# The first mean stage of a four-layer graph network: h computed by nodes in one product, with its bias, instead of by features and then turned

## What is computed

```python
# layer 2 and the norm behind it
out = fts @ W_l.T + aggregate @ W_r.T
out = out / norm(out, axis=1)
x = _layernorm(x + out)
# layer 3 starts with
h = x @ lin_w.T + lin_b
```

## Time and profile before

| | us |
|---|---|
| median of 3 runs | 5813.14 (5809.81 to 5825.58) |
| the profiled execution, its own time | 5838.2 |
| its span, from first to last instruction | 5836.3 |
| TensorE (PE) busy | 4153.4 |
| VectorE (DVE) busy | 3937.3 |
| POOL busy | 3517.6 |
| ScalarE (ACT) busy | 2806.0 |
| mean granted TensorE clock | 0.87 of full |

### The profile page before, as it was taken

How to read it: one execution, slowest core, us unless ns; L and a number is a source line. 1 busy time by engine, 2 the same in 40 slices (tenths; PEclk the granted TensorE clock), 3 DMA queues, 4 the chain that set the end, 5 groups by cost and what they waited for, 6 DMA issues and landing times. The chain is left out here.

```text
span 5836.3 us, 75364 instructions
## 1 busy us (share of the span) xinstructions
PE 4153.4 (71%) x16190; PEld 2475.1 (42%) x16190; DVE 3937.3 (67%) x13570; ACT 2806.0 (48%) x6338; POOL 3517.6 (60%) x3137
## 2 busy tenths in 40 slices
PE   5666649999994556466664779967996679756654
PEld 2333335555552333244442445534443334346643
DVE  6567759999995444277774885557666888746533
ACT  0434438788881100176663445534444555446543
POOL 4676658888866888545555650056105858855455
PEclk8788869999997777688886999989998999878776
DMA  6223333333323344456664774467545667657521
GB/s 219 73 80 83 78 74 110 114 110 113 112 91 73 62 62 63 68 179 196 200 195 131 209 209 136 123 190 217 152 142 163 188 172 210 188 186 229 169 79 53
DMA packets 785242, 802.39 MB, mean 137 GB/s; under 512 B 138080, under 2 KB 551848, under 8 KB 784666
## 3 DMA queue, kind: packets, MB, share of 16 engines
q1 hardware_dynamic: 403802, 393.43, 23.0%
q0 software_dynamic: 117504, 209.42, 14.9%
q10 hardware_dynamic: 263488, 194.72, 10.2%
HBM read 445.32 MB, written 351.92 MB: 137 GB/s over the span
## 5 line engine op out<-in xcount | busy, mean ns | idle before, releaser
L476 PE MATMUL gate_bank<-gate_ht,gate_whh 128*128 128x512 f32 x1764 | 884.9, 616 | 65.8 <-DVE gate_n L546 40.6
L942 POOL DMA_INDIRECT xh<-mean_xh,mean_pos_all x392 | 377.8, 964 | 342.5 <-DVE mean_xh L1008 209.6
L476 PEld LDWEIGHTS gate_bank<-gate_ht,gate_whh 128*128 128x128 f32 x1764 | 327.7, 197 | 469.3 <-issue 371.4
L2080 PE MATMUL back_ps_sums<-back_same,back_rows 128*128 128x512 f32 x400 | 288.8, 888 | 288.8 <-DMA back_rows<-x_a,back_idx 288.8
L1463 POOL DMA_INDIRECT ffn_rows<-att_sums,ffn_idx x392 | 394.4, 1006 | 124.0 <-issue 108.2
L291 POOL DMA_INDIRECT gate_rows<-h_a,by_pos x200 | 199.4, 997 | 428.9 <-POOLq L118 326.5
L472 PE MATMUL gate_bank<-by_rank,gate_win 128*128 128x512 f32 x882 | 435.3, 593 | 0.4 <-DVE by_rank L355 0.4
L612 ACT ACTIVATE gate_n<-gate_n,gate_b_ih 128x512 f32<-128x512 f32 x294 | 212.1, 722 | 397.0 <-issue 246.2
L1515 PE MATMUL ffn_ps_f<-ffn_hg,ffn_f 128*128 128x512 f32 x784 | 388.9, 597 | 3.0 <-ACT ffn_hg L1698 2.7
L1508 PE MATMUL ffn_ps_u<-ffn_xs_t,ffn_up_w 128*128 128x512 f32 x784 | 386.7, 595 | 1.1 <-issue 1.1
L2061 POOL DMA_INDIRECT back<-back_out,back_dest x200 | 324.4, 1622 | 67.8 <-issue 60.1
(11 more groups left out here) (270 smaller groups left out, 11751.2 us busy)
## 6 DMA issues: line engine op xcount, KB each, us to landing
mean_x<-x_a SPq DMA_DIRECT2D x196, 256.0 KB
back<-blank ACTq DMA_DIRECT2D x99, 264.0 KB, 4.4
mean_rows<-back SPq DMA_DIRECT2D x98, 264.0 KB
hp<-mean_xh SPq DMA_DIRECT2D x98, 264.0 KB
gate_x<-xh SPq DMA_DIRECT2D x98, 264.0 KB
gate_hot<-hot_rows SPq DMA_DIRECT2D x100, 256.0 KB
ffn_x<-in_x_in SPq DMA_DIRECT2D x98, 256.0 KB
ffn_xr<-in_x_in SPq DMA_DIRECT2D x98, 256.0 KB
```

What stands on the lines that cost most here:

```text
L476: last = nc.tensor.matmul(bank_[:, :], whh[:, c * D:(c + 1) * D], ht[:, t.slot4, :], start=not inputs, stop=True)
L942: nc.gpsimd.indirect_dma_start(out=g["xh"][:, :], out_offset=bass.IndirectOffsetOnAxis(ap=pos_all[:, t.n, j:j + 1], axis=0), in_=xh[:, t.n ...
L2080: last = nc.tensor.matmul(ps_sums[t.slot][:, :], rows[:, t.slot4, j, :], same[:, t.slot, j, :], start=j == 0, stop=j == J - 1)
```

## The change

h is made by nodes at once. TensorE first fills the bank `ps_h` with the bias by a product of a row of 128 ones (stationary, one partition) and lin_b repeated four times (moving, 1 x 512), then adds four products in which 128 turned rows of y are stationary and lin_w moves. ScalarE copies the bank into the finished row. The matmul by features, the bank `ps_ht`, the buffer `ht`, the turning back and VectorE's copy go. `ps_h` has two banks. The lags shrink: the columns 128 to 130 at 8 on VectorE (with the two setup copies that it makes ahead of tile 0's), the copy of h at 9 on ScalarE, POOL's indirect DMAs and the store of `hp` at 10. `lin_b` is loaded as one row of 512 floats in place of one number for each partition.

```diff
         @block.sync
-                if t := tile_at(11):
+                if t := tile_at(10):
                     wait(sp, id_done, t.n + 1)
                     wait_alone(sp, h_done, t.n + 1)
                     sp.dma_start(g["hp"]...)
         @block.gpsimd
-                if t := tile_at(11):
+                if t := tile_at(10):
         @block.tensor
             pe.wait_ge(w_loaded, 48)
+            pe.wait_ge(ones_set, 1)
...
                 if t := tile_at(8):
                     wait(pe, yt_done, t.n + 1)
-                    wait(pe, ht_done, t.n)
-                    nc.tensor.matmul(ps_ht[:, :], lin[:, :], yt[:, t.slot, :], start=True,
-                                     stop=True).then_inc(ht_made, 1)
-                if t := tile_at(9):
-                    wait(pe, ht_done, t.n + 1)
-                    wait(pe, h_done, t.n)
-                    for j in range(J):
-                        last = nc.tensor.transpose(ps_h[:, j * D:(j + 1) * D], ht[:, t.slot, j * P:(j + 1) * P],
-                                                   g["ident"][:, :])
-                    last.then_inc(h_turned, 1)
+                    wait(pe, h_done, t.n - 1)
+                    nc.tensor.matmul(ps_h[t.slot][:, :], ones[:, :], lin_b[:, :, :].rearrange("a j d -> a (j d)"),
+                                     start=True, stop=False, skip_group_check=True)
+                    for j in range(J):
+                        last = nc.tensor.matmul(ps_h[t.slot][:, j * D:(j + 1) * D], yt[:, t.slot, j * P:(j + 1) * P],
+                                                lin[:, :], start=False, stop=True, skip_group_check=True)
+                    last.then_inc(h_made, 1)
         @block.vector
+            nc.vector.memset(ones[:, :], 1.0).then_inc(ones_set, 1)
...
-                if t := tile_at(10):
-                    wait(dve, h_turned, t.n + 1)
+                if t := tile_at(8):
                     wait(dve, scattered[t.n % STAGED], 64 * (t.n // STAGED))
                     wait(dve, h_stored[t.n % STAGED], 16 * (t.n // STAGED))
...
                     nc.vector.tensor_copy(xh[:, t.n % STAGED, :, D:D + 3], tails[:, t.n, :, :]).then_inc(id_done, 1)
-                    nc.vector.tensor_copy(xh[:, t.n % STAGED, :, 0:D],
-                                          ps_h[:, :].rearrange("p (j d) -> p j d", j=J)).then_inc(h_done, 1)
         @block.scalar
                 if t := tile_at(9):
-                    wait(act, ht_made, t.n + 1)
-                    wait(act, h_turned, t.n - 1)
-                    nc.scalar.activation(ht[:, t.slot, :], ps_ht[:, :], ACT.Identity,
-                                         bias=lin_b[:, :]).then_inc(ht_done, 1)
+                    wait(act, h_made, t.n + 1)
+                    wait(act, scattered[t.n % STAGED], 64 * (t.n // STAGED))
+                    wait(act, h_stored[t.n % STAGED], 16 * (t.n // STAGED))
+                    nc.scalar.activation(xh[:, t.n % STAGED, :, 0:D],
+                                         ps_h[t.slot][:, :].rearrange("p (j d) -> p j d", j=J),
+                                         ACT.Copy).then_inc(h_done, 1)
                 if t := tile_at(8):
                     wait(act, y_turned, t.n + 1)
-                    wait(act, ht_made, t.n - 1)
+                    wait(act, h_made, t.n - 1)
                     nc.scalar.activation(yt[:, t.slot, :], ps_y[:, :], ACT.Copy).then_inc(yt_done, 1)
```

More of the change, by code:

```diff
@@ L899, in back_mean_pass @@
         lin = f.sb("lin", [P, D])
-        lin_b = f.sb("lin_b", [P, 1])
+        lin_b, ones = f.sb("lin_b", [1, J, D]), f.sb("ones", [1, P])
         yt = f.sb("yt", [P, 2, SUPER])
[L902 to L905, removed]
+        ps_y, ps_h = f.ps("ps_y"), [f.ps(f"ps_h{b}") for b in range(2)]
+        ones_set = f.sem("ones_set")
+        y_turned, yt_done, h_made, h_done = (f.sem(s) for s in ("y_turned", "yt_done", "h_made", "h_done"))
         block = ctx.enter_context(nc.Block())
@@ L911, in _ @@
             sp.dma_start(lin[:, :], g["lin_wt"]).then_inc(w_loaded, 16)
-            sp.dma_start(lin_b[:, :], column(g["lin_b"])).then_inc(w_loaded, 16)
+            sp.dma_start(lin_b[:, :, :], g["lin_b"].rearrange("(a b n) -> a b n", a=1, b=1).broadcast_to([1, J, D])
+                         ).then_inc(w_loaded, 16)
             sp.dma_start(ids[:, :, :], g["ids_t"]).then_inc(ids_loaded, 16)
@@ L927, in step @@
                                  xh[:, t.n % STAGED, :, 0:WIDE]).then_inc(h_stored[t.n % STAGED], 16)
-            over_tiles(sp, NT, 11, step)
+            over_tiles(sp, NT, 10, step)
             for b in range(STAGED):
@@ L945, in step @@
                             in_=xh[:, t.n % STAGED, j, :], in_offset=None).then_inc(scattered[t.n % STAGED], 16)
-            over_tiles(pool, NT, 11, step)
+            over_tiles(pool, NT, 10, step)
             for b in range(STAGED):
@@ L976, in step @@
                     wait(pe, yt_done, t.n + 1)
-                    wait(pe, ht_done, t.n)
-                    nc.tensor.matmul(ps_ht[:, :], lin[:, :], yt[:, t.slot, :], start=True,
-                                     stop=True).then_inc(ht_made, 1)
-                if t := tile_at(9):
-                    wait(pe, ht_done, t.n + 1)
-                    wait(pe, h_done, t.n)
+                    wait(pe, h_done, t.n - 1)
+                    nc.tensor.matmul(ps_h[t.slot][:, :], ones[:, :], lin_b[:, :, :].rearrange("a j d -> a (j d)"),
+                                     start=True, stop=False, skip_group_check=True)
                     for j in range(J):
-                        last = nc.tensor.transpose(ps_h[:, j * D:(j + 1) * D], ht[:, t.slot, j * P:(j + 1) * P],
-                                                   g["ident"][:, :])
-                    last.then_inc(h_turned, 1)
-            over_tiles(pe, NT, 9, step)
+                        last = nc.tensor.matmul(ps_h[t.slot][:, j * D:(j + 1) * D], yt[:, t.slot, j * P:(j + 1) * P],
+                                                lin[:, :], start=False, stop=True, skip_group_check=True)
+                    last.then_inc(h_made, 1)
+            over_tiles(pe, NT, 8, step)
         @block.vector
         def _(dve):
+            nc.vector.memset(ones[:, :], 1.0).then_inc(ones_set, 1)
             nc.vector.memset(xh[:, :, :, D + 3:WIDE].rearrange("p s j o -> p (s j o)"), 0.0).then_inc(tail_set, 1)
@@ L1045, in step @@
                     ln.statistics(nc, dve, t, [res[:, t.slot, j, :] for j in range(J)], y_done)
-            over_tiles(dve, NT, 10, step)
+            over_tiles(dve, NT, 8, step)
         @block.scalar
```

## The result

The kernel after takes 5836.45 us (median of 8 runs, 5826.69 to 5838.63), the kernel before beside it 5812.83 (8 runs): a ratio of 1.004 (95% interval 1.003 to 1.005), 24 us slower. The forecast was 5808, no change that can be measured. The time lies outside the forecast's own range of 5796 to 5826 and inside the wide one, 5745 to 5852, which took in the nearer rivals; the sign was wrong.

A forecast was written before the change was run, and what follows sets the result against it. It took mean1 to be bound by a ring of engines whose long steps wait for a PE count behind POOL's scatter. 49 pairs x (+0.1 - 0.1) - 4.7 = -5 us: 5833 profiled, 5808 as median, range 5796 to 5826.

The forecast's parts named there:

- Step 1: VectorE in mean1 loses the finished-row copy L1008, 0.60 us: its step falls from 5.57 to 4.97 us.
- step 2: ScalarE in mean1 loses L1062 and gains the copy of h from PSUM: 0 net.
- step 6: Start of mean1: h of tile 0 appears one step earlier, lag 9 in place of 10: -4.7 us, once.
- 5: Short steps of mean1: 6.05 us becomes 6.4 at half clock, 5.57 becomes 5.1 to 5.5 at full; 0.1 less in the mean.
- third rival: PE in mean1: turns, bias and products in one ring with `yt` decide at half clock; slower, 5852 us; chance 0.21.
- 49 pairs of a long and a short step: Steps of mean1 alternate, 7.54 and 6.05 us; 49 pairs x (+0.1 - 0.1) us entered the sum.
- step 3: PE in mean1 swaps L978 and four turns for eight matmuls and the bias product (1.02): net 0.46 us a tile, full clock.
- Point 4: Waits in mean1's long steps: POOL and SP wait for ScalarE's copy of h behind `xt`; 0.15 less or 0.3 more, taken +0.1 us.
- PE becomes the link: PE's burst in mean1 sets half the steps at half clock, 0.9 us more each: 44 less 5, 5852 us; chance 0.21.
- VectorE was the bound: VectorE in mean1: each tile falls by L1008's 0.60 us, 59, with the start 64: 5749 us; chance 0.29.
- The half clock goes: Busier PE in mean1 no longer falls to 0.50; 6.05 us steps become 5.57, with the start 29 less: 5784; chance 0.08.
- Every step becomes a long one: In mean1 h's count comes nearer POOL's batch; 98 x (7.54 - 6.75) = 77 us more: 5885; chance 0.04.

The follow-up runs named there:

- experiment 4: Kernel before with mean1 run twice, the second time without its indirect DMAs and landing waits: second stage costs 595 us on prompt chips, 585 on late chip 2.
- experiment 5: Kernel after with the bias product ahead of TensorE's wait for y and `yt` ahead of ScalarE's copy of h: 5850.0 us on a late chip, ratio 1.0034.

## Why the prediction was wrong

**Right.** What bounds the kernel (a ring of engines whose long steps end in a count held behind POOL's DMAs) stood, and experiment 4 showed it. That the count is one of PE's held only for the step in the earlier trace rows and 8 more; in most long steps it was VectorE's own. Step 1 (VectorE -57 us for -59), step 2 (ScalarE 0: copy 0.597 us, its busy time -16), and step 6 (-3.7 for -4.7) held.

**The step that failed is 5**, "I take 0.1 less in the mean". It gave a half-clock step 6.4 us; the trace has 7.21. I had let half clock reach only as far as in the earlier trace rows, so that the bias ended near 2575.8 and the products at 2576.9; the longer burst ran at half clock to its end. My own third rival had the arithmetic right: a burst of 5.8 at half clock plus 1.3 is 7.1, over the 5.1 that it may take. I had set it at 0.21, because at full clock the burst is short; but I hadn't followed what half clock does to the whole of it.

As an estimate, 18 such steps at 0.8 us more than the 6.4 are 15 of the 29 us between the forecast of -5 and the measured +24; the run with the copy on VectorE, which keeps as many, warns against taking that for the cause. The sum was also cast in 49 pairs of a long and a short step, and the change broke the pairs up: before, 43 steps of 7.5 us or more (mean 7.99) and 54 shorter ones (5.76); after, 25 of 7.7 or more (8.26), 27 of 7.05 to 7.4, and 45 shorter ones (5.82). And half clock became more frequent: 301 to 344 us between the first and the last copy of h in every late-chip kernel with the product by nodes, even without the bias (327), against 212 and 223 in the two stages of before. Why, no run tells.

A term of step 3 was small as well. The bias product was put at 1.02 and took 1.12, at half clock 2.07, and 146.6 us over the 98 tiles, 1.50 each. The lower clock did the rest of PE's +143 where 50 was forecast: even the product for v, which the change doesn't touch, rose from 114.3 to 137.2 us. That the bias product costs about the price of a full product is what the Trainium skill has in "TensorE: Matmul & The Clock Gate" (Part 2, step 3), and the traces agree to within an eighth: L979 contracts one row in 2.07 at half clock, L978 128 rows in 1.84.

**Point 4** was small in the same direction. It had +0.1 us in a long step for the copy's place behind `xt`. The run with the copy on VectorE puts the copy's place at some 18 us in all, the run without bias puts the bias at some 10; by their intervals each is uncertain by about 9, and the two overlap, since both act on the same steps, and after, copy and bias were timed on three different chips. That they add up to the 24 us and the 4 that the start gave back is in accord with this, not more. How the 18 us divide between `xt` ahead of a late copy and `yt` behind it was only argued; the order copy of h, `yt`, `xt` wasn't tried.

**The rivals.** "PE becomes the link" is nearest: its mechanism is in 18 of 97 steps, its sum was too large (+39 for +24), and experiment 5 shows that it isn't alone, for without it the pairs grow instead. "VectorE was the bound" is wrong here and right on prompt chips: it forecast 5749 from 5813, a ratio of 0.989, and these give 0.9886. "The half clock goes" is wrong on late chips: there the fuller PE had the lower clock, 0.76 for 0.85. The Trainium skill's rule ("TensorE: Matmul & The Clock Gate", "HAM oscillation"), that gaps without work drop the clock and a PE kept fed stays fast, isn't contradicted by that, since PE wasn't kept fed: it still waited 133.1 us for `yt`, 45 times, up to 5.2 us, as I had said of the gap of a long step. On the prompt chip, where its longest wait for `yt` is 2.6 us, the granted clock is 0.93. "Every step becomes a long one" didn't come.

One caution on the two profiles. The execution of before that I summed against was 25 us above its median, that of after lies on its own; so their stages differ by 3.7 us (717.3 and 713.6) where the medians differ by 24. On late chip 2 the same stage of before took 695.7 us. The 24 us seem to be lost in this stage all the same: in the traces of before, after and the four variants on late chips the span less the stage is 5114 to 5124 us, while the stage itself goes from 704.3 to 721.7. At its median of 5813 the kernel before would thus have a stage of some 687 to 697 us (an estimate from these spans), as on chip 2, and after's is 717. The period of such a stage moves from one execution to another, and only medians of many runs carry a verdict of 0.4%.

## What to carry to other kernels

When a stage's long steps end in a count that is late, ask which count it is and what holds it before costing any edit, and look at more than one such step: work saved ahead of it came to nothing here, and work put behind it or into the ring that restarts it (here ScalarE's copy, then `yt`, turns, bias, products) can cost more than was saved. Cost a burst on TensorE at the lower clock over its whole length if it starts there, and count a bias of one row as a full product. And time such a change on more than one chip: here it is 1.1% faster on some and 0.4% slower on others.

## What I had not expected

The same program takes 5476 us on three chips and 5809 to 5830 on three more, 6%. No execution of it lies between, and chip 6 was the same in two rounds. The indirect DMAs cost POOL the same on both (0.96 us an instruction). What differs is how late counts arrive behind them, an engine's own included: on late chips up to about 6.0 us after a batch of four begins, on prompt chips never noticeably. mean3, which the change doesn't touch, takes 6.55 us a tile in the earlier trace rows; on prompt chip 6 (the kernel without the bias, the same in mean3) its DMAs ran so:

```profile
L733 POOL DMA_INDIRECT out<-mean_y,node_at x196: 954/959/997, 5152.7 to 5399.1; - x196
```

(5399.1 + 1.0 - 5152.7) / 49 = 5.05 us, POOL's own pace. What makes a chip one or the other stays open; no run here tells.
